# RWKV token mixing moved from blended activations into the weights, with products of fp16 parts

## What is computed

```
def time_mix(x, mix):                      # x is normalised, x_prev is x one token earlier, zero at the first
    return x * mix + x_prev * (1 - mix)    # mix: one value for each channel

k = time_mix(x, time_mix_k) @ W_k.T
v = time_mix(x, time_mix_v) @ W_v.T
r = sigmoid(time_mix(x, time_mix_r) @ W_r.T)
wkv = scan over tokens of (k, v, time_decay, time_first)
mixed = (r * wkv) @ W_o.T
```

## Time and profile before

| | us |
|---|---|
| runs | 1509.42, 1508.44, 1513.4 |
| median | 1509.42 |
| span of the profiled execution | 1507.2 |
| PE busy in the span | 1317.1 (87%) |
| DVE busy | 1289.1 (86%) |
| ACT busy | 987.5 (66%) |
| POOL busy | 321.9 (21%) |
| `rwkv_phase`, ACT's first to the first MoE matmul | 1106.0 to 1296.9 |

### The profile page before, as it was taken

The page is one execution under the profiler, slowest core; times in us unless marked ns, Lnnn a source line. Parts: engine busy times, 40 slices in busy tenths (PEclk is TensorE's granted clock), DMA queues, the critical chain, the costliest instruction groups (busy, mean ns, idle before and its releaser), DMA issues. The chain is left out here.

```text
span 1507.2 us, 27409 instructions
## 1 busy us (share of the span) xinstructions
PE 1317.1 (87%) x9558; PEld 598.0 (40%) x9558; DVE 1289.1 (86%) x2289; ACT 987.5 (66%) x1292; POOL 321.9 (21%) x574
## 2 busy tenths in 40 slices
PE   4776999999999999999999986999767767789987
PEld 2454223232232332223322212766634334477754
DVE  6896999999999999999999932799879999865668
ACT  3452355888888888888888886666356655356642
POOL 3220000110102111020110202323100077300475
PEclk9897688999999999999999998999978889999999
DMA  6887412141423304242043024596354145686776
GB/s 207 274 258 212 58 33 45 21 81 27 83 46 43 83 7 79 46 79 49 10 78 73 12 48 116 170 316 197 133 181 140 49 167 181 223 259 204 232 230 190
DMA packets 158521, 186.16 MB, mean 124 GB/s; under 512 B 18228, under 2 KB 134708, under 8 KB 157364
## 3 DMA queue, kind: packets, MB, share of 16 engines
q1 hardware_dynamic: 135384, 151.45, 37.6%
q0 software_dynamic: 6144, 16.79, 3.6%
q10 hardware_dynamic: 16864, 16.26, 3.1%
HBM read 100.81 MB, written 83.36 MB: 122 GB/s over the span
## 5 line engine op out<-in xcount | busy, mean ns | idle before, releaser
L1332 DVE TENSOR_REDUCE att_m_part<-att_mx 128x1 f32<-128x512 f32 (+3 forms) x1152 | 680.4, 652 | 29.9 <-PE att_mx L1400 14.1
L1362 ACT ACTIVATE att_prob<-att_score,late_score_scale 128x1024 f32<-128x1024 f32 (+3 forms) x640 | 595.6, 987 | 166.9 <-PE att_score L1439 164.9
L1400 PE MATMUL att_mx<-early_kop,early_qop 48*128 48x512 f16 (+3 forms) x1280 | 354.4, 367 | 23.2 <-DVE att_neg_m L1311 6.0
L1422 PE MATMUL att_pv<-att_prob,early_v 128*32 128x512 f32 (+3 forms) x2560 | 305.5, 550 | 2.0 <-POOL att_prob L1299 2.0
L1439 PE MATMUL att_score<-early_qop,early_kop 50*128 50x512 f16 (+3 forms) x1280 | 253.2, 358 | 10.5 <-ACT att_prob L1362 9.4
L1400 PEld LDWEIGHTS att_mx<-early_kop,early_qop 48*128 48x128 f16 x1280 | 98.5, 94 | 374.5 <-DVE att_m_part L1332 346.9
L1299 POOL TENSOR_SCALAR_AFFINE_SELECT att_prob<-att_prob 128x256 f32<-128x256 f32 x256 | 102.9, 407 | 670.8 <-ACT att_prob L1362 669.9
L2215 PE MATMUL rwkv_prod<-rwkv_xm,late_mixT 128*128 128x512 f32 x192 | 98.6, 668 | 30.6 <-ACT rwkv_kvr L2169 20.5
L1439 PEld LDWEIGHTS att_score<-early_qop,early_kop 50*128 50x128 f16 x1280 | 72.0, 94 | 72.5 <-ACT att_prob L1362 56.5
L2437 POOL DMA_INDIRECT moe_yg<-results,routing_slot_i x64 | 64.2, 1004 | 126.1 <-issue 122.1
L1975 POOL DMA_INDIRECT rows<-rwkv_xs,routing_slot_i x64 | 66.5, 1039 | 114.6 <-DVE routing_slot_i L2067 95.5
(11 more groups left out here) (261 smaller groups left out, 1764.8 us busy)
## 6 DMA issues: line engine op xcount, KB each, us to landing
va<-qkv_v SPq DMA_DIRECT2D x8, 1024.0 KB, 6.4
early_v<-va SPq DMA_DIRECT2D x8, 1024.0 KB, 7.0
routing_xp<-parts SPq DMA_DIRECT2D x32, 256.0 KB, 3.7
moe_xt<-rows SPq DMA_DIRECT2D x30, 256.0 KB, 3.4
rows<-att_zeros SPq DMA_DIRECT2D x8, 928.0 KB, 6.5
early_kop<-qk SPq DMA_DIRECT2D x48, 128.0 KB, 4.4
results<-moe_y ACTq DMA_DIRECT2D x24, 256.0 KB, 3.0
results<-blend_x ACTq DMA_DIRECT2D x22, 256.0 KB, 2.6
```

Source lines behind the costliest of these rows:

```text
L1332: nc.vector.tensor_reduce(cells[:, sides[0]:sides[-1] + 1, some], mx[:, banks[0]:banks[-1] + 1, 0:len(hps) * w].rearrange("p a (h w) -> p ...
L1362: nc.scalar.activation(prob[:, r % (PROBS * HP), :, n0:], score[:, r % 2, :, n0:], ACT.Exp, scale=late_weights.score_scale[:, 0:1])\
L1400: op = nc.tensor.matmul(bank[:, n * w:(n + 1) * w], qop[rows, slot, t, hp, i * P:(i + 1) * P], kop[rows, slot, hp, c * GT:c * GT + w], sta ...
L1422: op = nc.tensor.matmul(pv[at, n0:], v[:, slot, j, at], prob[:, (st * HP + h // 2) % (PROBS * HP), h % 2, n0:], start=(j == 0), stop=(j == ...
```

## The change

The blend is linear, so it is moved into the weights. `MixedWeights` makes for each of k, v and r two weight matrices, one for the token itself (rows scaled by `mix`) and one for the token before (rows scaled by `1 - mix`), brings them to a common power-of-two scale and splits each into a high and a low fp16 part. A product is then a contraction over two tokens: 2 taps x 2 channel halves, each as three fp16 matmuls (high x high, low x high, high x low), on the fp16 parts of x, with the tap chosen by an offset of one element. `past`, `blend` and `xm` are gone, `kvr`'s copy out of PSUM takes `unscale` as its scale. `xn1T` and `ln_full` are gone too; x is loaded from `parts1` in two transfers. The x buffers' first column is cleared once by POOL. The load of x for group n now waits for `prod_done` of group n - 2.

Ahead of `means` DVE finds the scale and makes the parts, with two small matmuls on PE between products of attention (the fifth and sixth after the last maximum). To make room, the raw QKV weights are staged in `by_cos`, the raw RWKV matrices in the memory of the parts, and `hid_p` of the MoE phase takes over the parts' memory.

```diff
 class LayerNorm:
     def high(self, nc, act, n, slot):
         act.wait_ge(self.turn_done.sem, self.turn_done.done(n))
-        if self.full is not None:
-            nc.scalar.copy(self.full[:, slot], self.turned[:, :, :])
         nc.scalar.copy(self.hi[:, slot], self.turned[:, :, :]).then_inc(self.hi_done.sem, 1)
...
+class MixedWeights(PowerScale):
+    def bound(self, nc, dve, loaded, copied):
+        dve.wait_ge(*loaded)
+        dve.wait_ge(*copied)
+        nc.vector.tensor_scalar(self.by[:, :, self.BEFORE], self.by[:, :, self.NOW], -1.0, 1.0, ALU.mult, ALU.add)\
+            .then_inc(self.bounded, 1)
+        nc.vector.tensor_reduce(self.most[:, :, :], self.rows[:, :, :, :], AX.X, ALU.max, apply_absolute_value=True)
...
+    def divide(self, nc, dve):
...
+        for w in range(self.NW):
+            for s in range(2):
+                for k in range(KC):
+                    op = nc.vector.tensor_scalar(self.parts[:, 0, w, s, k], self.rows[:, w, k],
+                                                 self.shared_by[:, w, s, k:k + 1], None, ALU.mult)
+            op.then_inc(self.split, 1)
+        for w in range(self.NW):
+            dve.wait_ge(self.split, 2 + w)
+            for s in range(2):
+                for k in range(KC):
+                    op = nc.vector.scalar_tensor_tensor(self.parts[:, 1, w, s, k], self.rows[:, w, k],
+                                                        self.shared_by[:, w, s, k:k + 1], self.parts[:, 0, w, s, k],
+                                                        ALU.mult, ALU.subtract)
+            op.then_inc(self.split, 1)
...
 def attention_phase(...):
...
             nc.vector.reciprocal(rden[:, :], den[:, :]).then_inc(rden_done, 1)
+            mixed.bound(nc, dve, (late_weights.mixing_in, late_weights.MIXING), (late_weights.copied, mixed.NW))
+            mixed.vector(nc, dve, mixed_turn, mixed_spread, ident)
+            mixed.divide(nc, dve)
             late_weights.means(nc, dve)
...
+                if i == behind[TURN_BEHIND]:
+                    mixed.tensor_turn(nc, pe, mixed_turn, ident[:, :])
+                if i == behind[TURN_BEHIND + 1]:
+                    mixed.tensor_spread(nc, pe, mixed_spread, mixed_ones)
...
 class BlendInputs:
     def __init__(self, s):
-        self.x = s.sb("x", [P, B, KC, GT + 1])
+        self.flat = s.sb("x", [P, B * 2 * KC * (GT + 1)], F16)
+        self.x = self.flat[:, :].rearrange("p (b a k t) -> p b a k t", b=B, a=2, k=KC)
...
+    def load(self, eng, parts_d, n):
+
         b, use = n % B, n // B
-        eng.dma_start(self.x[:, b], xnT_d[:, :, b, use * GT:use * GT + GT + 1]).then_inc(self.x_in[b], 16)
+        at, first = b * T + use * GT, 1 if use == 0 else 0
+        for part in range(2):
+            eng.dma_start(self.x[:, b, part, :, first:], parts_d[part, :, :, at - 1 + first:at + GT])\
+                .then_inc(self.x_in[b], 16)
...
 def rwkv_phase(...):
...
             def load_x(n):
-                after(sp, xm_done, NW * (n - B + 1))
-                blended.load(sp, xnT_d, n)
+                after(sp, prod_done, NO * (n - B + 1))
+                blended.load(sp, parts_d, n)
...
-            def blend(n):
-                b = n % B
-                for w in range(NW):
-                    dve.wait_ge(prev_done, n * NW + w + 1)
-                    for c in range(KC):
-                        op = nc.vector.scalar_tensor_tensor(xm[:, b, w, c], x[:, b, c, 1:], mix[:, w, c:c + 1],
-                                                            xm[:, b, w, c], ALU.mult, ALU.add)
-                    op.then_inc(xm_done, 1)
-
...
-                    if c == 0:
-                        pe.wait_ge(xm_done, n * NW + w + 1)
+                    if o == 0:
+                        pe.wait_ge(x_in[b], blended.LOADED * (n // B + 1))
                     after(pe, kvr_done, n * NO + o + 1 - PRODS)
-                    for k in range(KC):
-                        op = nc.tensor.matmul(prod[:, (n * NO + o) % PRODS], wT[:, w, k, c * P:(c + 1) * P], xm[:, b, w, k],
-                                              start=(k == 0), stop=(k == KC - 1))
-                    op.then_inc(prod_done, 1)
+                    cols = slice(c * P, (c + 1) * P)
+                    taps = [(s, k) for s in (mixed.NOW, mixed.BEFORE) for k in range(KC)]
+                    parts_matmul(nc, prod[:, (n * NO + o) % PRODS],
+                                 [tuple(mixed.parts[:, part, w, s, k, cols] for part in range(2)) for s, k in taps],
+                                 [tuple(x[:, b, part, k, 1 - s:1 - s + GT] for part in range(2)) for s, k in taps])\
+                        .then_inc(prod_done, 1)
```

154 lines of the change are left out of this document (90 added, 64 removed).

## The result

Over 11 runs each the changed kernel takes 1517.7 us (1513.7 to 1523.5) and the kernel before 1509.42 (1507.0 to 1514.1). The ratio is 1.0053, with a 95% interval of 1.0042 to 1.0065: slower by 8.0 us, where 3.5 were forecast. The range (1504.5 to 1518) held the time, by 0.3 us. The profiled execution of the changed kernel is one of its fastest: 1514.15 us, span 1512.4. One kept trace of the experiments, e9's, is of a slow execution (1610.7 us, where the fast ones of that kernel take 1579.9 to 1596.0), so no finding rests on its trace.

What follows compares the result with a forecast made beforehand. DVE was taken to bound rwkv_phase, with the loop's bound moving to PE and POOL ending last. Span 1507.2 + 3.5 + 0.2 - 0.2 = 1510.7 us, plus 2.2 to the median: 1512.9 us, range 1504.5 to 1518.

Steps and rivals of the forecast that it cites:

- Products on PE: In rwkv_phase: 72 matmuls a group at 0.2167 us, 15.6 us, make PE's step 19.1 us, longer than DVE's 16.0.
- Rival B: Products in rwkv_phase cost PE no more than before, 10.3 us a group: 1500.6 us; chance 0.03.
- rival C: PE streams fp16 x operands beginning at an odd element at half pace, 7.8 us a group: 1571 us; chance 0.05.
- The new wait on SP: Early rwkv_phase: group 3's x load waits for products(1) and holds up the routing loads queued behind it, 5.8 us.
- Rivals A: Rival A: the new wait on SP is mostly hidden, the MoE phase starts 2.2 us earlier: 1507.2 us; chance 0.12.
- rival D: Loads of x, twice as many rows of half size, take 3 us more before the routing loads: 1516 us; chance 0.12.
- `slot_i`: In rwkv_phase: DVE writes it, releasing POOL's scatters, at 1211.1 us, 9.8 us later than before.
- DVE's end: End of rwkv_phase: DVE needs 82.6 us after slot_i, three blends fewer, and is done at 1293.7 us.
- It just fits: Late rwkv_phase: PE has group 7's second output at 1258.3 us and DVE asks for it at 1259.1, so no wait.
- POOL's end: End of rwkv_phase: POOL, ending 2.6 us after its last scatter's issue, had 6.2 us slack; now last, MoE starts +3.5 us.
- The end of attention: Before ffn_phase: DVE's added 15 us hides in 40.25 us of idle time; PE's two tiny matmuls add 0.2 us.
- Rival E: ffn_phase gains what ACT is spared, -2.6 us, together with rival A's -2.2: 1504.6 us; chance 0.08.

Runs made afterwards that it cites:

- e9: Changed kernel with the scale's two small matmuls eight places further back among the products at the end of attention; 1.0040 of the kernel before.
- e4: Changed kernel with two of the three part products (high weights with low parts of x left out); 1.0020 of the kernel before.
- e1: Changed kernel with the load of x for group 3 moved behind the routing inputs on SP; 1.0013 of the kernel before.
- e6: Changed kernel without the last 8 of the 64 scatters, on a chip of 1510.3 us; one run, 1508.0 us.
- e5: Kernel before with places moved behind the next step's blend on DVE, on a chip of 1510.3 us; one run, 1513.6 us.
- e10: Changed kernel run once more, unaltered, on a chip where the kernel before takes 1580.9 us; 1.0117 of the kernel before.
- e7: Kernel before with the routing taken earlier (choice ahead of step 3's blend, places ending step 3), no new buffers; 1.0025 of the kernel before.
- e8: Changed kernel with choice ahead of state(2), places in step 3, group 3's x load behind the routing inputs, no new buffers; 0.9952 of the kernel before.
- v1: Changed kernel with all routing inputs in eight buffers, loaded at the phase's start, and logits, choice and places made early; 0.9897 of the kernel before.

## Why the prediction was right and where it was wrong

**Products on PE**: right. 0.2167 us for a matmul and 19.04 us for a step; e4 shows that both groups ahead of the logits count in full. Rival B is out: 24 matmuls fewer take 5.2 us off a group, as 0.2167 says. The 131 ns that the Trainium skill gives in "TensorE: Matmul & The Clock Gate", Back-to-back issue gap, were not reached in any trace; its other figure there, some 216 ns for one matmul by itself, is what these streams show.

**Operands at an odd element** (rival C): no price. The halves with both taps run at 0.2167 us a matmul, the same as the MoE phase's.

**The new wait on SP**: right, in size (5.82 us for 5.8) and in cause (e1). Rivals A and D fall with it. What was not seen is that the rows for the scatters now hang on PE as well (e1).

**`slot_i`**: right, within 1.0 us. The clock of the first group cost 2.6 us and not 2.0, and products(1) ended 0.9 us late.

**DVE's end**: 3.2 us later in the phase than forecast, 190.95 for 187.7. One of them is `slot_i`'s; from `slot_i` on DVE took 84.9 us and not 82.6, 1.5 of them in three waits for PE and ACT in the last groups (0.90, 0.35 and 0.23 us), which the forecast had at nothing with "It just fits". The rest stays open. It did not decide the result, since POOL was later still, but it leaves the change without a gain even if POOL's end had cost nothing: e6 has 191.6 us, and the kernel before 190.9.

**POOL's end**: POOL was the last engine, as forecast, but the term for its end was mis-sized, and this is the step that failed: "A scatter lands 2.6 us after issue, which puts POOL's end at about 1290.0", and from it "only 6.2 us of slack". The landing was right. POOL's end is later, because its block ends with a drain of 5.295 us, 4.64 with eight scatters fewer. The slack was 2.2 us and not 6.2, so 4.0 of the missing 6.35 us are this. The others: `slot_i` 1.0 us later in the phase than forecast, and the scatters themselves 87.1 us and not 85.7 (0.7 of it in the first, 2.12 us and not 1.45). `slot_i` is 10.7 us later than before: 10.7 + 1.4 - 2.2 = 9.9, where 9.85 were measured. The bounds that I gave the landing, nothing to twice 2.6, did not reach the cost, since they were bounds of the wrong quantity: of one transfer, and not of what the engine does between its last instruction and the next phase. The row that would have warned me is one of the kernel before: POOL's first MoE row with [9.55 <-POOLq L1834] says only that the wait was longer than the landing; as other engines were late as well, it bounds POOL's end from above at 9.55, and that bound belonged into the range.

**The end of attention**: forecast at +0.2 us, it is -1.5 in the first pair of traces, and 1.2 us lie between the traces in which PE's clock falls there and those in which it doesn't. That fall was in the trace of before (0.78), and I priced only the two matmuls' own length. What keeps the clock up is not shown (e9).

**`ffn_phase`**: -0.6 in the first pair, -0.2 forecast; over all traces it is 183.1 to 185.8 with the change and 184.4 to 186.1 without it, so it is hardly more than its scatter. Rival E's 2.6 us did not come.

**The sum.** The direction of the likeliest time was right and its size less than half, 3.5 of 8.0. That the range held is luck: 1517.7 lies 0.3 us inside an upper end that was made of a landing of twice 2.6 us and of slower loads (rival D), and neither came. The time came near it by the drain, which no term covered. A forecast with the slack at 2.2 would have been 3.5 + 4.0 = 7.5 us, 1516.9, in what the prediction calls slower, with a chance of 0.38, as is the measured time.

## What to carry to other kernels

Where an engine issues indirect transfers and a phase ends with a barrier, count behind its last transfer not the landing alone but the engine's own drain, 5.3 us for 64 scatters here; the first row of the next phase on that engine bounds it. A change that takes work off the bounding engine pays only when the next chain is moved too: here the early routing gave nothing in the kernel before (1.0025, on one chip), and with one load moved it took the changed one from 1.0117 (1.0040 by e9) to 0.9952 there, and with eight buffers to 0.9897 on a chip of 1510 us. And where a load's wait is tied to another event, read what is queued behind it: one line of order on SP was worth 6.4 us of `slot_i`.

## What the runs showed of the hardware

**POOL's drain** was 5.295 us behind 64 scatters in twelve traces and 4.64 behind 56 in two. These are two points; that it goes with the number is read from them and from the 0.05 us at the end of `qkv_phase`.

**A landing** of the last scatter came 2.4 us after its issue in the traces of before and after, and 4.8 us in e5.

**On two of the three chips PE's instructions come slowly while the scatters run.** Windows of e10 (busy us of PE, PEld, DVE, ACT, POOL, PEclk, DMA share, GB/s):

```profile
1215.00:1237.00 22.00, 20.95 (x97) 10.62 (x95) 21.51 (x28) 7.94 (x10) 17.13 (x17) 1.00 0.50 173
1237.00:1260.00 23.00, 11.65 (x22) 2.22 (x22) 3.23 (x3) 3.24 (x4) 14.13 (x15) 0.54 0.45 154
1260.00:1289.00 29.00, 28.58 (x126) 14.68 (x125) 26.94 (x32) 15.99 (x19) 22.34 (x21) 0.96 0.51 172
1289.00:1306.00 17.00, 5.84 (x11) 1.13 (x11) 3.77 (x5) 1.27 (x2) 11.53 (x12) 0.63 0.30 108
```

For 23 and 17 us PE gets through 22 and 11 matmuls, where 97 and 126 stand in the stretches beside them, and its idle time is put down to "issue": it waits for nothing that the profile shows. The weight loads come at steps of some 0.70 us or multiples of it:

```profile
1241.27 0.10 PEld L102 LDWEIGHTS rwkv_prod<-blend_x,late_mixed_parts 128*128 128x128 f16 x1 [1.26 <-issue]
1242.01 0.10 PEld L102 LDWEIGHTS rwkv_prod<-blend_x,late_mixed_parts 128*128 128x128 f16 x1 [0.63 <-issue]
1243.40 0.10 PEld L102 LDWEIGHTS rwkv_prod<-blend_x,late_mixed_parts 128*128 128x128 f16 x1 [1.28 <-issue]
```

The kernel before has it on these chips too, with few and long gaps (e7, PE in the same part of the phase):

```profile
1222.70 6.09 PE L2215 MATMUL rwkv_prod<-rwkv_xm,late_mixT 128*128 128x512 f32 x8 [7.40 <-issue]
1244.51 3.72 PE L2226 MATMUL rwkv_out_ps<-late_mixT,rwkv_y 128*128 128x256 f32 x8 [15.71 <-issue]
1255.63 3.78 PE L2215 MATMUL rwkv_prod<-rwkv_xm,late_mixT 128*128 128x512 f32 x4 [5.68 <-issue]
1268.26 3.75 PE L2215 MATMUL rwkv_prod<-rwkv_xm,late_mixT 128*128 128x512 f32 x4 [8.85 <-issue]
```

These are 37.6 us together, and the phase is 38 us longer there than in the kernel before at 1510 us; the MoE phase is another 35 us longer. In the traces of e1, e7, e8 and e10 all such gaps of `rwkv_phase` lie between the first scatter and some 4 us after the last. What slows PE's instructions, and why on these chips only, no run here tells; it stays open. It is likely why the same edits weigh differently there: the early routing without buffers made 0.5% on the chip of 1581 us, and v1 made 1.0% on one of 1510.
